# A decoder layer in one kernel: the orders of work behind attention step 14 written out anew

## What is computed

```python
dist = where(ed < 0.1, dist_taylor, where(ed > 2.0, dist_asymp, dist_standard))
o = softmax(causal(-beta * dist)) @ v
x = x + o @ Wo.T
log_D = cs[:, :, :, None] - cs[:, :, None, :] + igate      # cs: running sum of log_sigmoid(fgate)
D = exp(log_D - max_log_D)
C = (q @ k.T) / sqrt(dh) * D                                # q: norm(x), k and v: the context
hs = (C / max(|sum C|, exp(-max_log_D))) @ v
x = x + headnorm(hs) * scale
probs = top-2 of softmax(norm(x) @ router.T), renormalised
x = x + sum_e probs[e] * ((silu(h @ gate_e) * (h @ up_e)) @ down_e)      # h: norm(x)
```

## Time and profile before

| what | us |
|---|---|
| median of three runs | 253.34 |
| the three runs | 253.34, 254.0, 250.28 |
| the profiled execution | 250.77 |
| its span | 249.0 |
| PE, DVE, ACT, POOL busy | 197.5, 188.8, 156.9, 112.3 |
| granted clock of PE, mean | 0.842 |

### The profile page before, as it was taken

One profiled execution on the slowest core, in us unless ns is written; L12 is line 12 of the kernel. 1 busy time (PEld: TensorE's weight loads), 2 busy tenths in 40 slices (PEclk: granted clock), 3 DMA queues, 4 the chain that ended last, 5 costly groups with the idle time before them and its releaser, 6 DMA issues.

```text
span 249.0 us, 6399 instructions
## 1 busy us (share of the span) xinstructions
PE 197.5 (79%) x2341; PEld 151.3 (61%) x2341; DVE 188.8 (76%) x532; ACT 156.9 (63%) x319; POOL 112.3 (45%) x151
## 2 busy tenths in 40 slices
PE   0697542685777584897899877999999898999994
PEld 0354231464655463685566632578889787898884
DVE  5868899999999999987685499564877843656554
ACT  2399979999999997963464221774555658332320
POOL 9730354685665455626153045002577556743000
PEclk9999955559587778555599587999999999999999
DMA  4304574867294179100004000000000000100001
GB/s 120 94 2 101 164 208 133 214 155 194 72 314 141 34 220 324 27 3 0 4 3 162 9 1 0 3 0 0 0 3 3 0 3 0 42 4 0 0 3 43
DMA packets 28252, 17.43 MB, mean 70 GB/s; under 512 B 11572, under 2 KB 26300, under 8 KB 27964
## 3 DMA queue, kind: packets, MB, share of 16 engines
q1 hardware_dynamic: 28220, 17.01, 24.5%
HBM read 12.03 MB, written 4.92 MB: 68 GB/s over the span
## 4 chain that ended last, share of the span: by engine, by line
PE 45%; DVE 27%; issue 13%; ACT 11%; DMA 1%; DVEq 1%; ACTq 0%
PE P L1359 31%; PE PO L1359 12%; DVE nm L1037 4%; DVE dist L1078 3%; PE PM L1359 3%; DVE dist_mem L1025 3%; DVE xn L958 2%; DVE dist_mem L1043 2%; DVE nm L1070 1%; DMA x_sb<-x 1%; ACT split_mem L725 1%; DVE wgu L984 1%; DVE dist_mem L1018 1%; DVE split_mem L1137 1%; ACT split_mem L841 1%
## 5 line engine op out<-in xcount | busy, mean ns | idle before, releaser
L1320 DVE SCALAR_TENSOR_TENSOR dist_mem<-P,gub,dist_mem 128x512 f32<-128x512 f32 x32 | 23.8, 749 | 24.7 <-ACT dist_mem L880 24.4
L880 ACT ACTIVATE dist_mem<-P,gub 128x512 f32<-128x512 f32 x32 | 21.9, 689 | 30.8 <-PE P L1359 30.8
L614 POOL TENSOR_SCALAR m_gt<-dist_mem 128x640 uint8<-128x640 f32 x16 | 29.3, 1831 | 5.5 <-issue 3.8
L1359 PEld LDWEIGHTS PO<-proj_mem,dist_mem 128*128 128x128 f32 x244 | 29.4, 192 | 1.2 <-DVE ctx_sb L1338 0.2
L1359 PE MATMUL PO<-proj_mem,dist_mem 128*128 128x128 f32 x244 | 30.0, 276 | 0.0
L1359 PE MATMUL P<-cf,dist 128*128 128x128 f32 x80 | 22.8, 367 | 6.7 <-ACT shift L808 6.7
L1359 PE MATMUL P<-xhi,whi 128*128 128x512 f32 x64 | 26.5, 414 | 1.1 <-DVE dist_mem L1320 1.1
L603 POOL TENSOR_TENSOR dist<-dist,cf 128x128 f32<-128x128 f32 x16 | 7.3, 458 | 40.8 <-DVE dist L1078 40.8
L1359 PE MATMUL P<-xhi,wlo 128*128 128x512 f32 x64 | 25.0, 391 | 0.0
L1359 PE MATMUL P<-xlo,whi 128*128 128x512 f32 x64 | 25.0, 390 | 0.0
L1359 PEld LDWEIGHTS P<-cf,dist 128*128 128x128 f32 x80 | 14.8, 185 | 12.3 <-ACT shift L808 9.7
(11 more groups left out here) (255 smaller groups left out, 521.2 us busy)
## 6 DMA issues: line engine op xcount, KB each, us to landing
q_split<-split_mem SPq DMA_DIRECT2D x16, 128.0 KB, 2.5
k_split<-split_mem SPq DMA_DIRECT2D x4, 512.0 KB, 3.7
stq<-q_split SPq DMA_DIRECT2D x16, 128.0 KB
stk<-k_split SPq DMA_DIRECT2D x16, 128.0 KB
split_mem<-no_rows SPq DMA_DIRECT2D x1, 1024.0 KB, 5.2
wgu<-gate_w SPq DMA_DIRECT2D x1, 1024.0 KB, 5.9
wgu<-up_w SPq DMA_DIRECT2D x1, 1024.0 KB, 9.9
dist<-no_rows SPq DMA_DIRECT2D x1, 1024.0 KB, 5.0
```

The lines of the kernel that those rows point to most:

```text
L614: pool.tensor_scalar(m_gt[:, g.k % 2, :], e2[:, g.k % 2, :], 4.0 - ATT_EPS, None, ALU.is_gt).then_inc(sm["gt_done"], 1)
L880: A(sil[:, f, :], (P1, P2)[f][:, 0, :], ACT.Silu, bias=gub[:, 0, one:one + 1]).then_inc(sm["sil_done"], 1)
L1320: V.scalar_tensor_tensor(hT[:, z % 2 * 2 + f, :], (P1, P2)[f][:, 1, :], gub[:, 1, one:one + 1], sil[:, f, :], ALU.add, ALU.mult).then_inc( ...
L1359: return nc.tensor.matmul(out_, lhsT, rhs, start=start, stop=stop, **more)
```

## The change

The steps of PE, ACT and DVE now end at 14 (`LAST_STEP`), and what steps 15 to 20 and place (21, 1) did is written out in a function `tail()` of each engine, as a list of calls. For that the pieces of `step` became functions of their own (`values`, `maxima`, `turned`, `joined`, `projected`, `exponent`, `outputs`, `taken`, `lowest`, and so on) with the waits they had. Apart from this:

- The context's gate product of the first half (`of_context(0)`) moves ahead of step 14's scores, the rows' one (`of_rows(0)`) behind step 14's turning.
- The last three units' `nm` goes through P2 bank 1 in place of PM (`top_bank`).
- `outs(m)` writes to P2 bank 1 or to PM by turns for the first half (`cross_bank`) and waits for `hs_done` m - 1 in place of m.
- The transposition of normed rows waits for each of its four rows (`xn_done`), not for all four.
- `qk(4)` waits for `hs_done` 4 in place of `x1_done` 8; ACT's `outs(4)` waits for `hvar_done` and `hn_done`.
- `stay_warm` writes to PO, and 8 of its matmuls are left (`WARM = (3, 5)`), ahead of `qk(5)` and of `qk(6)`.
- `outs(6)` is issued behind `gate_up(0)`.
- POOL does `blocks(0)` and `centre(0)` behind all of its steps; `blocks(0)` stood at step 14.

```diff
-DVE_AT = {...
-          (18, 7): [("rows", 2), ("rows", 3)],
-          (20, 1): [("stat", 6)],
...
-WARM = (7, 5, 2, 6, 1, 0)
+WARM = (3, 5)
+LAST_STEP = 14
...
-            return P2[:, 1, :] if m < CB else P3[:, 1, :]
+            return (P2[:, 1, :], PM[:, :])[m % 2] if m < CB else P3[:, 1, :]
...
-                pe.wait_ge(sm["xn_done"], CB * (n + 1))
                 for b in range(CB):
+                    pe.wait_ge(sm["xn_done"], CB * n + b + 1)
...
-                wait(pe, "hs_done", m)
+                wait(pe, "hs_done", m - 1 if 0 < m < CB else m)
...
-                if s == 14:
-                    blocks(0)
-                if s == POOL_CENTRE:
-                    centre(0)
+            blocks(0)
+            centre(0)
...
-            steps(step, -2, NU + 4)
-            at(M0 - 1, 1)
+            def tail():
+                u = {k: At(None, k) for k in range(NU)}
...
+                projected(u[11])
+                front(0, 5)
+                values(u[14])
+                ex(0)
+                values(u[15])
+                qk(0)
+                joined(u[14])
+                joined(u[15])
+                projected(u[14])
+                ex(1)
+                projected(u[15])
+                of_context(1)
+                qk(1)
+                outs(0)
+                ex(2)
...
+                front(1, 4)
+                outs(2)
+                front(1, 5)
+                outs(3)
+                ex(4)
...
+            steps(step, -2, LAST_STEP)
+            tail()
```

## The result

| | before | after |
|---|---|---|
| median, us (21 executions each, taken in turn) | 251.82 | 249.45 |
| lowest and highest, us | 250.23, 254.0 | 246.12, 253.28 |
| ratio with its 95% interval | | 0.987 (0.984 to 0.990) |
| the profiled execution, us | 250.77 | 253.28 |
| its span, us | 249.0 | 251.5 |

The change saves about 1%, 2.4 us by the medians. The single times say more: before lies within 4 us, the kernel after spreads over 7, in two loose groups, eleven executions up to 249.45 us and ten from 250.69 on. The profiled one is the slowest of them all.

The account below looks back on a forecast made before the run. Ahead of the first expert matmul, waits of one chain on the next bound the kernel: +3.4 - 5.0 - 3.9 = -5.5, with +1.0 for `outs(6)` and +1.0 for POOL, -3.5 us. From 252.1 that gives 248.6 us, range 244.5 to 254.0.

Parts of the forecast that it names:

- First part: Up to the last Wo product: PE's dense list ends at 131.5, last statistics at 132.3 us, 9 us earlier than before.
- Second part: From there to the head norm: postponed products and gate hops put it at 144.75 us, 3.4 us later than before.
- `front(1, 4)` ahead of `outs(2)`: Second half's gate hops: PE must pass the transposition before issuing head product 2, whose operands are ready since 137 us.
- Third part: Head norm to logits: without the interleaved gate chain DVE needs 9.6 us, not 14.6; logits copied at 159.3, not 162.0.
- A clock of 0.5 between 131 and 150: Sign against the forecast: the granted clock at half between 131 and 150 us, ahead of the experts.
- the five cases: Clock up near 131 us (0.35), staying down (0.24), rising late (0.22), rising early (0.15), or reorder not reaching the end (0.04).
- the rival of the early clock: Ahead of the experts: clock rises by 125 us, 3.5 us more saved, 245.1 us; chance 0.15.
- the rival of the low clock: Clock stays down: second part 5.2 us dearer, third up to 2 more, 253.8 to 255.8 us; chance 0.24.
- The logits and `gate_up(0)`: Ahead of the experts: logits copied near 159 us and `gate_up(0)` directly behind, where `outs(6)` and others stood before.
- `outs(6)`, +1.0: Experts' stretch: moved behind the first expert matmul, it costs PE there what it cost ahead, 0.97 us.
- POOL, +1.0: Second half's gate chain: POOL's SBUF work beside it stalls DVE, costing 1.0 us, bounds 0 and 3.0.
- the sign looked for, 0.5 us and more on 16 columns: Sign against the forecast: DVE operations of 0.5 us and more on 16 columns between 138 and 144 us.

Follow-up runs that it names:

- x1: The changed kernel run again with no edit, for a second trace and as partner of its variants: median 249.72 us, ratio to before 0.981.
- y2: The changed kernel with the unused products of both x3 and y1: median 246.13 us, ratio to before 0.978.
- x3: The changed kernel with seven more unused 512-column matmuls, ahead of the second half's gate sum and transposition: median 246.97 us, ratio to before 0.982.
- x2: The changed kernel with head product 6 and ACT's copy of it back ahead of the first expert unit: median 251.39 us, ratio to before 1.000.
- x4: The changed kernel with head product 2 ahead of the second half's gate sum and transposition on PE: median 250.58 us, ratio to before 0.997.
- y4: x4 with four of x3's unused products, ahead of the second gate step: median 249.15 us, ratio to before 0.987.
- z3: y2 with the normed rows' transposition, router product and logits' copy put first, no unused products behind the router product: median 246.19 us, ratio to before 0.977.
- y3: x3 with POOL's split of the third expert unit's weights held until the second half's row statistics are spread: median 248.41 us, ratio to before 0.989.
- y1: The changed kernel with eight unused 512-column matmuls around the first expert unit: median 247.86 us, ratio to before 0.987.
- z2: y2 with the first half's cross products back in one bank, each waiting for ACT's copy of the one before: median 247.83 us, ratio to before 0.984.
- w1: z3 with head product 7 moved behind the second expert unit's first products: median 244.59 us, ratio to before 0.970.

## Why the prediction was right, and where it was not

The median is 249.45 us where 248.6 was predicted, inside the range, and the change is within 2% of before. It started from 252.1 for before, which measured 251.82, and took off 3.5 us; the medians differ by 2.4. The sum can be held against three traces. Each term is a difference to before, in us, from the marks above (for before: 103.96, 141.36, 155.96, 164.82, 246.34 and 250.77):

| term | predicted | after | x1 | y2 |
|---|---|---|---|---|
| start of the region | 0 | +1.10 | -0.39 | +0.65 |
| normed rows to head norm | +3.4, +1.0 for POOL | +3.97 | +3.99 | +2.44 |
| head norm to end of normed rows | -5.0 | -3.73 | -3.91 | -5.03 |
| end of normed rows to first expert matmul | -3.9 | -3.75 | -3.75 | -3.95 |
| first expert matmul to the last DVE operation | +1.0 | +3.88 | +0.72 | +1.24 |
| from there to the end of the device time | 0 | +1.04 | +1.06 | +0.03 |
| sum | -3.5 | +2.5 | -2.3 | -4.6 |

**First part: right in its end, wrong in its inside.** The turning of unit 12 begins at 111.72 (111.5 predicted), the last Wo product at 131.49 (it was to end at 131.5), and the last statistics end at 132.85 (132.3). Less the 1.10 us by which this execution was late, the last statistics are 0.5 us earlier than predicted, and the last attention result comes 26.95 us behind the normed rows in place of 36.65. But the clock had risen already at 127.13 and not near 131, so four of those microseconds ran faster than counted. PE's waits made up for it: it is busy only 14.31 of the 17.06 us up to 127.13, where the sum had 0.8 us of waits in all. Two errors of opposite sign met.

**Second part: right in its number, by luck.** The head norm was to come 3.4 us later than before by the orders, and 4.4 with POOL; counted from the normed rows it came 4.0 later in both traces. That number holds a low clock, which the walk didn't have: head products 2 and 3 took 1.81 and 1.92 us where 0.9 each had been counted. With the clock up until the head norm was all but reached it came 2.4 to 2.5 later (y2 2.44, x3 2.42, x2 2.53). So the walk was too long by 1 us without POOL and by 2 with it, and the clock put back most of that. The step that it named, `front(1, 4)` ahead of `outs(2)`, is real but small: x4 against x2 and y4 against x3 give 0.5 and 0.4 us for it.

**Third part: right in the work, wrong in the clock.** DVE's 9.6 us from head norm to the end of the rows is 9.57 in y2, at full clock. In after and x1 it is 10.87 and 10.69, since PE was at 1.2 GHz until 154.44 and 152.60, and DVE waited 1.35 us for its `qk` product at 154.79. "A clock of 0.5 between 131 and 150" was named as what would prove the case wrong, and it happened, from 140.78 and 139.00 on. So none of the five cases came as it was told: the clock rose as early as the rival of the early clock had it, or nearly (127.13 and 125.34), and then fell again ahead of the head norm. It cost less than the rival of the low clock had been given: x1 needs 2.9 us more than y2 from the normed rows (57.19 against 54.32), where 5.2 to 7.2 had been reckoned for both parts.

**The logits and `gate_up(0)`: right.** 4.9 to 5.1 us remain from the rows to the first expert matmul (5.0 predicted), and nothing stands between the logits' copy and it. z3 shows that 1.7 us of this was still queueing.

**`outs(6)`, +1.0: near in size, wrong in its reason.** It takes 0.98 us behind the first unit's products, and x1 is 0.72 us longer from the first expert matmul on. But x2 shows that without it PE waits there for ACT's `wtsT` instead, 1.40 us in place of 0.25. So it was not PE's work that was given back. In before the bias products start 4.31 us behind the first expert matmul with no such wait, with the router's chain already further on: its logits were copied 2.82 us ahead of that matmul, and 0.39 in the kernel after.

**POOL, +1.0: a stall of that size, but not on the path.** The 16-column operations of the forget gate kept to 0.16 to 0.21 us (so the sign looked for, 0.5 us and more on 16 columns, did not come there), but the running maxima took 1.52 us in after and 1.62 in x3, where they take 0.60 when POOL stands still (y3): 0.9 to 1.0 us. In after and x1 DVE then waited 1.46 us for ACT's copy of head product 3 all the same, so the head norm would not have come earlier without the stall. y3 shows the same at full clock: maxima 1.0 shorter, first step of the head norm 0.18 earlier. The first half's maxima were stalled too, 1.81 us in after against 0.60 in before; the prediction didn't look there. The rule of the Trainium skill (SBUF — State Buffer, Who interferes with whom) that a DVE instruction with two SBUF inputs and a GpSimd instruction that reads SBUF exclude each other for the whole instruction, agrees with y3, where a DVE operation of 0.19 us took 1.19 and ended 0.05 us after POOL's.

**What the sum lacked: the clock among the experts, and the end.** The prediction took the expert stretch as PE's own work at full clock. x1 and y2 have it so. In the profiled execution of the kernel after the clock fell for 6.8 us in the first two units, and that is 3.16 us: head product 7 at 1.88 us for 1.08 (x1 at full clock), and the twelve products of the second unit at 0.57 to 0.77 for 0.39 to 0.47. The end of the kernel took 1.0 us more in both traces, which no term had. y1 speaks for the narrow products as what the fall hangs on: 512-column products put around them, and nothing else changed, took the executions above 250 us away. With unused products among the experts (y1, y2, z2, z3, w1, six executions each) none of 30 is above 249.3 us; without them (x1 to x4, y3, y4) 31 of 48 are, and still 27 if 1.0 us is taken off the times of x1, x2 and x4 for their longer end. But the clock fell among the experts in z2 and z3 as well, for 3.4 us in place of 6.8, so the unused products made it shorter or rarer and did not rule it out. How many of the 21 executions had the fall isn't known; only two of this kernel were profiled, one with it (253.28) and one without (248.49). That the median came within 0.9 us of the prediction is in part the meeting of errors: the gain was smaller than counted in the third part and at the end, and the cost smaller in the second part.

**What stays open.** Why x2 and x4 have no execution below 249.7, while the kernel after has eleven, isn't settled; no run separated the position of the narrow products in time from their share of the work. Nor is it settled why the end of the kernel is 1.0 us longer in the traces of after, x1, x2 and x4, or what the 252.25 of x3 and the 248.03 of w1 are.

## What to carry to other kernels

When a reorder packs chains more densely, price the stretch behind it too: the first two units of the experts cost 3.2 us more in one of two traces of the same kernel, by the clock alone. Before a difference between two traces is put down to an edit, look for a trace of the same order whose clock fell at the same place: x4 looked like 1.95 us until x2 stood beside it, and is 0.49. Look at all single times before trusting one trace; a spread that grew from 4 to 7 us said more than the ratio. Work that is moved out of a wait saves nothing (x2). A stall that two engines share over memory is only moved by delaying one of them (y3); it has to be put where the other engine has a wait.

## What the runs showed of the hardware

- The granted clock fell while PE was busy nearly without a gap: in the kernel after PE worked 5.44 of the 5.69 us ahead of the fall at 168.10, part of it on products of 33 columns, 8 rows deep or 128 columns wide. After the fall it was busy 6.82 of 6.82 us at 1.2 GHz. With eight unused products of 512 columns and bf16 around them y1 kept 2.4 GHz over the whole 85.38 us; z2, with the same eight, was at 1.2 GHz from 166.0 to 169.4.
- In the profiled execution of z3, 11 products between 164.00 and 167.40 ran at 1.2 GHz; with one group of eight 33-column products moved behind the next twelve wide ones (w1) the profiled execution had none.
- A DVE operation of two SBUF operands that meets a POOL subtraction of 1.26 us takes as long as that has left: 0.19 us became 1.19, and two of 0.30 became 1.62.
